# Many-headed attention in a fused eight-layer kernel: the scores computed a second time with keys on partitions

## The reference

```python
x = x + jnp.tanh(g_xattn[2]) * _L2_xattn_ref(_layernorm(x, axis=-1), ctx_1024, ctx_1024, mask_BxS2_bf1, ...)

def _L2_xattn_ref(q, k, v, key_padding_mask, Wq, bq, Wk, bk, Wv, bv, Wo, bo):   # 16 heads of 16 features
    qh = (q @ Wq.T + bq).reshape(B_, Lq, N_HEADS, D_HEAD).transpose(0, 2, 1, 3)
    kh = (k @ Wk.T + bk).reshape(B_, Lk, N_HEADS, D_HEAD).transpose(0, 2, 1, 3)
    vh = (v @ Wv.T + bv).reshape(B_, Lk, N_HEADS, D_HEAD).transpose(0, 2, 1, 3)
    scores = jnp.einsum('bhqd,bhkd->bhqk', qh, kh) / jnp.sqrt(jnp.float32(D_HEAD))
    scores = jnp.where(key_padding_mask[:, None, None, :], scores, -jnp.inf)
    attn = jax.nn.softmax(scores, axis=-1)
    out = jnp.einsum('bhqk,bhkd->bhqd', attn, vh)
    return out.transpose(0, 2, 1, 3).reshape(B_, Lq, D) @ Wo.T + bo
```

## Time and profile before

| | |
|---|---|
| median of the runs | 3073.4 us |
| profiled execution, first to last instruction | 3069.1 us |
| TensorE, its weight loads busy | 2945.7 us (96%), 2275.7 us |
| VectorE, ScalarE, GpSimd busy | 2030.9, 1448.5, 650.4 us |
| mean granted TensorE clock | 0.973 of full speed |
| the many-headed layer, first score product to last | 1974.23 to 2635.73 us |

### The profile page before, as it was taken

How to read it: one execution, slowest core, us unless ns; L and a number is a source line. 1 busy time by engine, 2 the same in 40 slices (tenths; PEclk the granted TensorE clock), 3 DMA queues, 4 the chain that set the end, 5 groups by cost and what they waited for, 6 DMA issues and landing times. The chain is left out here.

```text
span 3069.1 us, 61161 instructions
## 1 busy us (share of the span) xinstructions
PE 2945.7 (96%) x23332; PEld 2275.7 (74%) x23332; DVE 2030.9 (66%) x4378; ACT 1448.5 (47%) x2845; POOL 650.4 (21%) x952
## 2 busy tenths in 40 slices
PE   8997999989899999999999999799999999899999
PEld 6874656567799999999999999577777777556444
DVE  5773111138577887788888877566767666589664
ACT  3431111126455555555555555476666666556000
POOL 4565000046100220013012200212212112036000
PEclk9997999999899999999999999899999999899999
DMA  9643233249300000000000000000000000337100
GB/s 292 214 128 106 82 117 110 88 144 299 104 1 2 1 2 1 2 1 1 2 1 2 1 2 1 24 25 22 17 22 22 17 22 17 106 108 227 51 14 21
DMA packets 79537, 185.47 MB, mean 60 GB/s; under 512 B 12981, under 2 KB 23202, under 8 KB 78916
## 3 DMA queue, kind: packets, MB, share of 16 engines
q1 hardware_dynamic: 62708, 141.50, 14.3%
q10 hardware_dynamic: 10208, 25.30, 2.8%
q0 software_dynamic: 6336, 14.76, 1.7%
HBM read 150.26 MB, written 27.79 MB: 58 GB/s over the span
## 5 line engine op out<-in xcount | busy, mean ns | idle before, releaser
L2792 DVE CUSTOM_DVE_ANT_0 probs<-ps,add 112x375 f32<-112x375 f32 x512 | 258.9, 544 | 82.7 <-PE ps L2945 76.0
L2871 ACT ACTIVATE probs<-probs,neg_top 112x375 f32<-112x375 f32 x512 | 278.5, 600 | 63.5 <-DVE neg_top L2792 60.1
L1734 DVE TENSOR_TENSOR hidden<-gated,ps 128x512 f32<-128x512 f32 x64 | 44.0, 687 | 294.7 <-PE ps L1777 294.7
L2972 PEld LDWEIGHTS ps<-ident,probs 112*125 112x125 f32 x1536 | 196.8, 188 | 44.4 <-issue 16.7
L2351 DVE TENSOR_REDUCE top<-ps 112x16 f32<-112x1792 f32 x96 | 194.2, 2023 | 46.1 <-PE ps L2590 45.9
L2972 PE MATMUL ps<-ident,probs 112*125 112x112 f32 x1536 | 219.7, 279 | 1.8 <-DVE probs_t L2799 1.8
L3416 PE MATMUL ps<-we,xn_t 128*128 128x512 f32 x448 | 201.9, 614 | 1.7 <-PEq L846 0.9
L2367 DVE TENSOR_TENSOR probs<-probs,inv_sum 112x1792 f32<-112x1792 f32 x96 | 196.0, 2042 | 3.3
L2355 DVE TENSOR_TENSOR probs<-ps,top 112x1792 f32<-112x1792 f32 x96 | 194.3, 2024 | 3.3
L2363 DVE TENSOR_REDUCE row_sum<-probs 112x16 f32<-112x1792 f32 x96 | 193.9, 2020 | 3.2 <-ACT probs L2475 3.2
L2558 PE MATMUL ps<-ident,probs 112*112 112x112 f32 x1536 | 179.8, 260 | 8.2 <-ACT probs_t L2470 7.3
(11 more groups left out here) (464 smaller groups left out, 6276.8 us busy)
## 6 DMA issues: line engine op xcount, KB each, us to landing
ctx_t<-in_ctx_T_dram SPq DMA_DIRECT2D x96, 375.0 KB, 4.5
ctx_sb<-in_ctx_dram ACTq DMA_DIRECT2D x64, 384.0 KB, 4.5
ctx_sb<-in_ctx_dram SPq DMA_DIRECT2D x32, 384.0 KB, 8.9
ctx_sb<-in_ctx_T_dram SPq DMA_DIRECT2D x32, 375.0 KB, 3.1
queue<-zeros SPq DMA_DIRECT2D x32, 256.0 KB, 5.1
rows<-queue SPq DMA_DIRECT2D x16, 512.0 KB, 4.9
outputs<-out SPq DMA_DIRECT2D x16, 512.0 KB, 2.9
mask_in<-in_mask_BxSxS_fk_dram SPq DMA_DIRECT2D x16, 328.1 KB
```

Of the source, the lines that this page charges most:

```text
L2792: dve.tensor_tensor_reduce(out=probs[:, u, h, :], in0=k.ps[0:S, SCORE + h, 0:L], in1=add[:, j % 2, :], scale=1.0, scalar=BIG, op0=ALU.add, ...
L2871: act.activation(probs[:, u, h, :], probs[:, u, h, :], ACT.Exp, bias=neg_top[:, u, h:h + 1], scale=-1.0).then_inc(s["probs_done"], 1)
L2972: mm = pe.transpose(k.ps[0:KR, PT + h % 2, r * S:(r + 1) * S], probs[:, n % 3, h, r * KR:(r + 1) * KR], k.ident[0:S, 0:S])
```

## The change

After the change the probabilities are never transposed. The scores with queries on partitions (`scores`) are made as before, and VectorE takes only their minima, over two heads (two banks) an instruction, into a tile `top` that is zero but for one column in each strip of 32. TensorE transposes `top` (`transpose_top`), and VectorE adds the result to the unit's queries (`add_top`), which puts the minimum into one of the strip's rows that belong to the other head and were zero. A second product (`shifted`) then has the keys as its weights, three chunks of 125 for each of four heads, and these queries as its moving operand, and gives scores with keys on partitions: the keys' rows for the other head hold -1 where the queries have the minimum, so it is subtracted, and the pad mask (0 or 1e30) where the queries have 1. ScalarE takes the exponential of two banks at once, 125 x 672, straight into the tile that `attend` reads.

For this the keys are kept twice (one copy a parity, with the other head's rows set by scale and bias: -1, and 0 elsewhere), and the mask row is written into these copies by 16 loads a batch, of one row each, from a small tensor in DRAM that the layer before fills. `mask_q` becomes four instructions for two. `copy_raw` copies after every unit instead of every fourth. PSUM has a ring of six banks for scores and shifted scores, of which a unit uses four (the second half of a unit's banks are the next unit's first half), SMALL, and one bank for attended values, transposed minima and late side blocks. In a turn TensorE runs `scores` of n, `attend` of n - 2, a side block, `shifted` of n - 1, a side block, `transpose_top` of n. The side blocks are the same products, partly in other turns, and the loop starts four turns earlier.

```diff
@@ many_headed_storage, searched_network
+    m.pads = k.ctx_sb[0:B, 6, :, :].rearrange("p r d -> p (r d)")[:, D:D + L]
+    m.pad_in = k.ctx_sb[0:B, 7, 2, 0:L // 4 + 1].bitcast(U8)[:, 0:L]
...
+                sp.wait_ge(m.s["pads_ready"], 1)
+                sp.dma_start(k.pad_rows[:, :], m.pads).then_inc(m.s["pads_stored"], 16)
...
+                pool.tensor_scalar(m.pads, m.pads, -PAD, PAD, ALU.mult, ALU.add).then_inc(m.s["pads_ready"], 1)
@@ many_headed_attention: SyncE
+                    for a in range(DC):
+                        sp.wait_ge(s["k_copied"], DC * j + a + 1)
+                        for r in range(PARITIES):
+                            first = HD2 * (1 - r) + 1
+                            for h in range(UNIT):
+                                sp.dma_start(k_t[VW * h + first:VW * h + first + 1, j % 2, a, r, :], k.pad_rows[j:j + 1, :]).then_inc(pad_rows_loaded[j % 2], 16)
+                    if j + 2 < B:
+                        sp.wait_ge(s["v01_done"], j + 1)
+                        sp.wait_ge(s["v2_done"], j + 1)
+                        sp.dma_start(w.ctx_t[j % 2], k.ctx_t_dram[j + 2]).then_inc(w.ctx_t_loaded[j % 2], 16)
@@ VectorE
-                def mask_scores(n, half):
-                def copy_even(n, h):
...
+                def find_tops(n):
+                    parity = n % PARITIES
+                    tops = top[:, parity, :].rearrange("p (h w) -> p h w", w=VW)[:, :, HD2 * (1 - parity)]
+                    dve.wait_ge(s["scores_done"], n + 1)
                     if n >= 2:
+                        dve.wait_ge(s["top_transposed"], n - 1)
+                    for i in range(2):
+                        at = bank(n, 2 * i)
+                        dve.tensor_reduce(tops[:, 2 * i:2 * i + 2], k.ps[0:S, at:at + 2, 0:L], AX.X, ALU.min).then_inc(s["tops_found"], 1)
+                def add_top(n):
...
+                    dve.tensor_tensor(q_top[:, n % 2, :], k.ps[:, ATT, TOP:TOP + S], q_t[:, j % 2, a, parity, :], ALU.add).then_inc(s["q_topped"], 1)
@@ VectorE, order in a turn
+                    if u == 3 and 0 <= j - 1 < B:
+                        norm_att(j - 1)
                     if 0 <= n < N:
+                        find_tops(n)
...
+                    if 0 <= n < N:
+                        add_top(n)
@@ ScalarE
+                def exp(n):
+                    act.wait_ge(s["shifted_done"], n + 1)
                     if n >= 2:
                         act.wait_ge(s["att_done"], n - 1)
+                    for i in range(2):
+                        at = bank(n, 2 * i)
+                        act.activation(probs_t[:, n % 2, 2 * i:2 * i + 2, :], k.ps[0:KR, at:at + 2, 0:KC * S], ACT.Exp, scale=-1.0).then_inc(s["probs_done"], 1)
...
                 def copy_k(j, a):
+                    for r in range(PARITIES):
+                        ins = act.activation(k_t[:, j % 2, a, r, :], k.ps[:, SMALL, 0:L], ACT.Identity, bias=w.k_bias[:, a, r:r + 1], scale=w.k_keep[:, r:r + 1])
@@ TensorE
 scores(n)
+                    if u == 0:
+                        pe.wait_ge(pad_rows_loaded[j % 2], 16 * DC * PARITIES * UNIT * (j // 2 + 1))
                     if n:
-                        pe.wait_ge(s["logits_done"], UNIT * n)
+                        pe.wait_ge(s["tops_found"], 2 * n)
+                    if n >= 2:
+                        pe.wait_ge(s["probs_done"], 2 * n - 3)
+                def transpose_top(n):
+                    pe.wait_ge(s["tops_found"], 2 * n + 2)
...
+                    pe.transpose(k.ps[:, ATT, TOP:TOP + S], top[:, n % PARITIES, :], k.ident[0:S, 0:S]).then_inc(s["top_transposed"], 1)
+                def shifted(n):
+                    pe.wait_ge(s["q_topped"], n + 1)
+                    if n:
+                        pe.wait_ge(s["probs_done"], 2 * n)
+                    pe.wait_ge(s["tops_found"], min(2 * n + 3, 2 * N))
+                    for r in range(KC):
+                        for h in range(UNIT):
+                            rows = slice(h * VW, (h + 1) * VW)
+                            mm = pe.matmul(k.ps[0:KR, bank(n, h), r * S:(r + 1) * S], k_t[rows, j % 2, a, parity, r * KR:(r + 1) * KR], q_top[rows, n % 2, :], start=True, stop=True)
-                def transpose_probs(n, half):
...
+                    late_free(n)
                     if 0 <= n - 2 < N:
+                        attend(n - 2)
                     if u == 0 and 0 <= j - 2 < B:
                         project_out(j - 2)
+                    if u == 1 and new:
+                        project_q(j + 1)
+                    if u == 2 and 0 <= j + 2 < B:
+                        transpose_xn(j + 2)
+                    if u == 2 and new:
+                        project_v2(j + 1)
+                    if u == 3 and old:
+                        transpose_att(j - 1)
+                    if 0 <= n - 1 < N:
+                        shifted(n - 1)
+                    if u < 2 and new:
+                        project_k(j + 1, u)
+                    if u == 2 and old:
+                        transpose_raw(j - 1)
+                    if u == 3 and new:
+                        project_v01(j + 1)
+                    if 0 <= n < N:
+                        transpose_top(n)
```

More of the change, by code:

```diff
@@ L2722, in _ @@
             def _(sp):
-                sp.dma_start(w.pad[:, :], k.inputs["mask_BxS2_bf1"].rearrange("(a b) k -> a (b k)", a=1).partition_broadcast(S)).then_inc(w.pad_loaded, 16)
-                for j in range(2, B):
+                for j in range(B):
                     if j == 4:
@@ L2910, in _ @@
                     j, u = divmod(n, UNITS)
[L2911 to L2914 removed]
+                    new = 0 <= j + 1 < B
                     if 0 <= n - 2 < N:
[L2916 to L2920 removed]
@@ L2964, in attend @@
                     mm.then_inc(s["att_done"], 1)
-                def transpose_probs(n, half):
-                    for h in range(2 * half, 2 * half + 2):
-                        pe.wait_ge(s["probs_done"], UNIT * n + h + 1)
-                        if 2 * n + half:
-                            pe.wait_ge(s["odd_copied" if h % 2 else "even_copied"], 2 * n + half)
-                        for r in range(KC):
-                            mm = pe.transpose(k.ps[0:KR, PT + h % 2, r * S:(r + 1) * S], probs[:, n % 3, h, r * KR:(r + 1) * KR], k.ident[0:S, 0:S])
-                        mm.then_inc(s["head_transposed"], 1)
@@ new lines, in transpose_xn, with transpose_att @@
+                def transpose_xn(j):
+                    pe.wait_ge(s["normed"], j + 1)
+                    pe.wait_ge(s["q_masked"], j)
+                    for a in range(DC):
+                        mm = pe.transpose(late(S)[:, a, :], xn[:, j % 2, a * P:(a + 1) * P], k.ident[0:S, 0:S])
+                    mm.then_inc(s["xn_transposed"], 1)
+                def transpose_att(j):
+                    pe.wait_ge(s["att_normed"], j + 1)
+                    pe.wait_ge(s["xn_t_copied"], min(j + 4, B))
+                    if j == B - 1:
+                        pe.wait_ge(s["residual_done"], B - 1)
+                    for a in range(DC):
+                        mm = pe.transpose(late(S)[:, a, :], att[:, a * P:(a + 1) * P], k.ident[0:S, 0:S])
+                    mm.then_inc(s["att_transposed"], 1)
@@ new lines, in project_k @@
+                def project_k(j, a):
+                    if a:
+                        pe.wait_ge(s["k_copied"], DC * j + 1)
+                    else:
+                        pe.wait_ge(w.ctx_t_loaded[j % 2], 16 * (j // 2 + 1))
+                        pe.wait_ge(s["v01_copied"] if j else s["gbo_added"], max(j, 1))
+                    for c in range(DC):
+                        mm = pe.matmul(k.ps[:, SMALL, 0:L], w.wk_t[:, c, a * P:(a + 1) * P], w.ctx_t[j % 2][:, c, :], start=c == 0, stop=c == DC - 1)
+                    mm.then_inc(s["k_done"], 1)
@@ L3022, in transpose_raw @@
                     for u in range(UNITS):
[L3023 removed]
+                        mm = pe.transpose(k.ps[0:S, SMALL, u * P:(u + 1) * P], att_raw[:, j % 2, u, :], k.ident[:, :])
                     mm.then_inc(s["raw_transposed"], 1)
[L3026 to L3031 removed]
```

339 lines of the change are left out of this document (164 added, 175 removed).

## The result

| | before | after |
|---|---|---|
| time, median (range), us | 3073.5 (3073.2 to 3074.7) | 3025.1 (3022.2 to 3027.1) |
| span of the profiled execution, us | 3069.1 | 3022.4 |
| first to last score product of the stage, us | 661.5 | 615.6 |
| one batch in the steady stretch, us | 21.10 | 19.56 |

The change makes the kernel faster: 0.9846 of the time before, 95% interval [0.9833, 0.986], or 48.4 us. The forecast was 3013 in a range of 2985 to 3055. The direction and the mechanism held; 12 us of the forecast's 60 did not come.

What follows compares the result with a forecast made beforehand. TensorE, busy 96% of the span, was taken as the bound: 14.50 + 3.40 + 0.60 + 0.40 + 0.35 = 19.25 us a batch for 21.19; with ends +2.5 and -2 the stage loses 60.1 us, giving 3013 us, range 2985 to 3055.

Steps and rivals of the forecast that it cites:

- The second product, 0.85: TensorE's product with keys as weights: 0.85 us a unit, 3.40 a batch; ends 0.74 and 0.99.
- the row strips don't overlap: Rival on the second product: its 24 instructions run without overlap, 2.6 us a unit, kernel slower; chance 0.02.
- Tops, 0.15 each: TensorE's transposed maximum, one transpose a unit: 0.15 us each, 0.60 a batch; ends 0.11 and 0.29.
- Changes of shape, 0.40: TensorE switching between whole-array and tiled work: 8 more changes a batch at 0.05 us, 0.40; ends 0 and 0.76.
- 14.50 + 0.40: TensorE work kept in a batch, 21.19 less 6.69 us of probabilities' transposes, plus the changes of shape.
- The drains' rival: Mode changes at full price: eight at 0.19 us, 1.52 a batch for 0.40, kernel 3048 us; chance 0.09.
- Waits, 0.35: TensorE waits a batch: 0.2 us for the exponential (unit 2 to 3), 0.15 for unit 3's first minimum; ends 0 and 1.0.
- the 6.69 us that go: The probabilities' transposes on TensorE, 12 a unit, that the change removes: 6.69 us of a batch.
- the 9.2%: Batch falling from 21.19 to 19.25 us, applied to the stage's 661.5 us: 60.6 us less.
- the +2.5: Stage start: first scores wait for row loads and VectorE set-up, 2.5 us more; bounds 0 and 6.1.
- Mask-row loads, 0: SyncE's 16 one-row loads a batch: 6.1 us for eight against 8.1 of cover, so no cost.
- The 0.9 us a load of the rival: Late mask rows: loads served one after another, 10.8 us against 8.1, every batch waits 2.7, 3098 us; chance 0.10.

## Why the prediction was nearly right, and where the 12 us went

**What bounds the kernel.** Right. Halving either new operation of the chain gave back only the waits that the timeline shows; doubling the second product cost its work in every unit.

**The second product, 0.85.** Right to the hundredth, partly by luck: it was scaled from the earlier trace rows by count and by width, while the doubled product shows 0.655 of work and 0.195 paid once. It stands at 0.85 only because the order alternates over the strips. The forecast gave "the row strips don't overlap" 0.02 on the strength of the 31 ns in the earlier trace rows; a milder form of that mechanism is real (1.77 us where the rival had 2.6), but it hangs on the order, and the order was good. The Trainium skill, TensorEngine Tiling (Array Packing), Tiling Modes, Key Properties, says that different tiles can execute in parallel; the trace agrees (27 ns a record when the order alternates, 1.77 us for 24 records when it does not).

**Tops, 0.15 each: mis-sized.** This is the first failed term. It was halved from a pair of transposes followed by row strips, as if the pair's 0.29 were two equal pieces. One takes 0.19: 0.10 goes when it is left out, and 0.09 stays on the block ahead of the scores. Four a batch make 0.76 for 0.60, 0.16 us.

**Changes of shape, 0.40.** Right in sum, 0.05 each in the mean, but not block by block. Side blocks ahead of the second product or the transposed maximum grew: the output projection from 0.87 to 1.05, the key projections from 1.28 to 1.37 each, while the query projection (1.07 to 1.08) hardly did. That a long product ahead of a change hides part of it is thus not shown: behind the key projection 0.09 stayed, about the whole 0.095 that the forecast had read for one change. Kept work and changes together are 19.56 - 3.40 - 0.76 - 0.50 = 14.90, and the forecast had 14.50 + 0.40. The rule of the Trainium skill that a change of tiling mode drains the engine (TensorEngine Tiling (Array Packing), Tiling Modes, Key Properties) agrees with the 0.09 us that stayed on the key projection when the transpose behind it was left out. The drains' rival, 0.19 for each of eight, was too dear.

**Waits, 0.35: mis-sized, at the right two places.** They are 0.33 and 0.16 us in the timeline, and 0.28 and 0.16 went when the operation was halved. At the exponential the cover was about as forecast (0.49 us of raw transposes and 0.19 for 0.55 and 0.15) and the exponential shorter (0.73 for 0.83). What failed is the forecast's estimate of 0.1 for the two hand-overs: from the block behind the product (2299.32) to the next scores (2300.33) pass 1.01 us, and less the exponential that leaves 0.28. At the first minimum the size was right and the reason wrong: the minimum follows the scores at once, and scores with their hand-over (0.96), the minimum (0.94) and the hand-over to the product (0.15) come to 2.05 us, where TensorE has 0.83 + 0.72 + 0.34 = 1.89. Some 0.15 us too little in all.

So 0.16 + 0.15 = 0.31 us a batch, 31 batches, are 9.6 us. Another 0.09 x 31 = 2.8 us is the reference: the one batch of the earlier trace rows took 21.19 us, but the median of all batches of that trace, by the starts of their first scores, is 21.10, and it is the one batch above that. The second half of its first unit's transposes took 1.08 us where the next batch's takes 0.99, so the 6.69 us that go were 0.09 too many:

```profile
2330.51 0.81 PE L2972 MATMUL ps<-ident,probs 112*125 112x112 f32 x6
2331.50 1.10 PE L2988 MATMUL ps<-ctx_sb 128*125 128x256 f32 x4 [0.18 <-DVE x_sb L2821]
```

Some 2 us more are the first batch and the last units, to which the 9.2% were applied as if they were steady: the first batch became 0.9 us longer (16.12 to 17.05). Together the stretch gave 14.7 us less than the forecast's 60.6, and the ends gave 2.7 back.

**Ends.** From the stage's first instruction to the first scores pass 17.57 us, where it was 17.92: the +2.5 did not come, and that is luck. The set-up did cost: the first key projection waits 2.15 us for VectorE and starts 5.8 us after the stage's first instruction, where it was 4.2. But the granted clock, 0.50 (1.2 GHz) in both kernels when the stage begins, after TensorE had been idle for 8.5 us, stood at 1.00 (2.4 GHz) from about 1970.0 us, 12 us into the stage, where before it rose at about 1975.1, 19 us in and behind the first scores. So the eight records of the value projection ahead of the scores took 1.99 us instead of 3.78 (the first line is of the kernel before). Why it rose earlier is not shown.

```profile
1970.53 3.78 PE L3039 MATMUL ps<-ctx_sb 128*125 128x256 f32 x8 [0.67 <-ACT k_t L2885]
1963.92 2.84 PE L3093 MATMUL ps<-ctx_sb 128*128 128x375 f32 x4 [2.15 <-DVE ctx_sb L2877]
1973.45 1.99 PE L3118 MATMUL ps<-ctx_sb 128*125 128x256 f32 x8 [0.47 <-ACT v L2940]
```

The first scores waited 0.2 us for a mask row, once. From the last scores to the end, 2 us less, as taken. With these the stage lost 48.1 us (698.4 to 650.3) for 60.1 forecast.

**Mask-row loads, 0.** Right, as the run without them shows. The 0.9 us a load of the rival had no row; eight issues took 2.3 us, and no later batch waited.

## What to carry to other kernels

Where one engine works without a gap, price the change by that engine's work, group start to group start, and then look for the few places where the new chain has less cover than its longest operation; check which operation ends last there, not which is queued ahead, and price the hand-overs from a row. Take the steady unit from the median over many batches, and price a single small transpose by itself, with the change of shape behind it, not as half of a pair. When a product is only needed to choose a shift, it can be computed in a narrower type, and here that was worth as much as the change itself.

## What the runs showed of the hardware

- The order of row-tiled products decides how far they overlap: the same 24 records took 0.85 us alternating over four strips and banks and 1.77 us strip by strip.
- With the transpose ahead of the scores left out, 0.09 us stayed on the projection in its place (key projection 1.37 to 1.46, value projection 1.83 to 1.92); in the second product 0.195 us is paid once a group, whatever its length.
- A 32-row product of 375 columns in four strips took 0.83 us in float32 and 0.44 in bfloat16: a little over half, for half the records.
- The exponential over 125 x 672 from PSUM took 728 ns, less than the 0.83 us interpolated from the earlier trace rows; the minimum over 112 x 750 took 935, as interpolated.
- From the start of the block behind the second product to the exponential, and from its end to the next scores, 0.14 us pass each time, 0.28 together.
